# Wide tiles in the first feed-forward: two chunks of one image per operation of ScalarE, VectorE and GpSimd

## The reference, cut to what matters

```python
def _L0_conv_ref(x, gn_w, gn_b, w1, b1, w2, b2):
    # fft and inverse fft cancel; group norm with 8 groups, weight and bias
    xn = groupnorm(x, 8) * gn_w + gn_b
    h = relu(einsum('oc,bchw->bohw', w1, xn) + b1)
    return x + einsum('oc,bchw->bohw', w2, h) + b2

x = x + _L0(_gn(x))     # first feed-forward: the change is here
x = x + _L1(_gn(x))     # four sweeps: row by row, new = row + relu(conv9(prev) + b)
x = x + _L2(_gn(x))     # four sweeps
x = x + _L3(_gn(x))     # attention over channels, second feed-forward with gelu
```

## Time and profile before

| | |
|---|---|
| median of 3 runs | 2603.39 us |
| the profiled execution | 2601.79 us |
| its span, first to last instruction | 2600.0 us |
| TensorE busy | 2508.5 us (96%) |
| VectorE busy | 1809.3 us (70%) |
| ScalarE busy | 1238.0 us (48%) |
| GpSimd busy | 357.4 us (14%) |
| convolutions of the sweeps (line 883) | 2199.5 us, 40640 matmul records |
| granted TensorE clock, mean | 0.991 of full speed |

### The profile page before, as it was taken

The page is one execution under the profiler, slowest core; times in us unless marked ns, Lnnn a source line. Parts: engine busy times, 40 slices in busy tenths (PEclk is TensorE's granted clock), DMA queues, the critical chain, the costliest instruction groups (busy, mean ns, idle before and its releaser), DMA issues. The chain is left out here.

```text
span 2600.0 us, 116999 instructions
## 1 busy us (share of the span) xinstructions
PE 2508.5 (96%) x46072; PEld 2415.1 (93%) x46072; DVE 1809.3 (70%) x5768; ACT 1238.0 (48%) x2705; POOL 357.4 (14%) x551
## 2 busy tenths in 40 slices
PE   1999999999999999999999999999999999998998
PEld 1389999999999999999899999999999999997885
DVE  7866666666666666677666666666666666777986
ACT  0866663222233333377666642222333333676877
POOL 1610000000000000066100000000000000653545
PEclk9999999999999999999999999999999999998999
DMA  7810001222450000087700012223700000430006
GB/s 271 222 42 0 0 0 38 61 61 61 92 52 0 0 5 0 0 259 162 198 1 0 0 29 61 61 61 87 68 0 0 0 0 0 130 97 2 4 4 259
DMA packets 323834, 155.07 MB, mean 60 GB/s; under 512 B 155169, under 2 KB 319650, under 8 KB 319650
## 3 DMA queue, kind: packets, MB, share of 16 engines
q1 hardware_dynamic: 321600, 153.41, 23.1%
q10 hardware_dynamic: 2146, 0.53, 0.1%
HBM read 70.00 MB, written 50.33 MB: 46 GB/s over the span
## 5 line engine op out<-in xcount | busy, mean ns | idle before, releaser
L883 PE MATMUL banks<-x_row,w_taps 128*64 128x124 f32 (+2 forms) x40640 | 2199.5, 270 | 4.4 <-DVE x_row L1128 3.1
L883 PEld LDWEIGHTS banks<-x_row,w_taps 128*64 128x64 f32 x40640 | 2197.4, 135 | 6.5 <-issue 4.7
L1137 DVE SCALAR_TENSOR_TENSOR x_row<-banks,sweep_nbias,biased_row 128x128 f32<-128x128 f32 x2032 | 713.3, 351 | 713.1 <-PE banks L883 686.0
L668 ACT ACTIVATE biased_row<-state,sweep_bias 128x256 f32 (+1 forms) x762 | 512.8, 673 | 1038.3 <-DVE state L1140 605.2
L664 ACT ACTIVATE biased_row<-state,aff,gn_a 128x64 f32 (+1 forms) x1016 | 364.6, 430 | 183.4 <-DVE state L1146 179.6
L1140 DVE SCALAR_TENSOR_TENSOR state<-banks,sweep_nbias,biased_row 128x128 f32 (+1 forms) x1016 | 444.4, 437 | 0.0
L553 POOL TENSOR_TENSOR state<-state,stripe_a 128x256 f32<-128x256 f32 x96 | 66.9, 735 | 1979.6 <-DVE state L1140 1959.3
L1146 DVE SCALAR_TENSOR_TENSOR turn_ring<-banks,sweep_nbias,biased_row 128x64 f32<-128x64 f32 x1016 | 237.1, 275 | 0.0
L1146 DVE SCALAR_TENSOR_TENSOR state<-banks,sweep_nbias,biased_row 128x64 f32 (+1 forms) x1016 | 237.1, 275 | 0.0
L856 PE MATMUL banks<-res,ffn_w 64*64 64x512 f32 x512 | 112.3, 597 | 6.1 <-ACT res L603 5.2
L845 PE MATMUL banks<-state,ffn_s 64*64 64x512 f32 x512 | 107.1, 601 | 0.3 <-DVE ffn_s L1300 0.3
(11 more groups left out here) (139 smaller groups left out, 904.0 us busy)
## 6 DMA issues: line engine op xcount, KB each, us to landing
state<-turn_ring SPq DMA_DIRECT2D x512, 64.0 KB, 1.9
resid<-state SPq DMA_DIRECT2D x94, 256.0 KB, 3.6
state<-x_in SPq DMA_DIRECT2D x16, 1024.0 KB, 20.6
stripe_a<-resid SPq DMA_DIRECT2D x32, 512.0 KB, 5.4
stripe_b<-resid SPq DMA_DIRECT2D x32, 512.0 KB, 5.4
out_y<-state SPq DMA_DIRECT2D x16, 1024.0 KB, 4.0
res<-resid SPq DMA_DIRECT2D x32, 256.0 KB, 7.3
resid<-state SPq DMA_DIRECT2D x16, 512.0 KB, 6.5
```

The costliest lines, as they stand in the source:

```text
L668: nc.scalar.activation(as_cells(n, biased_row[:, k, :, :]), cells(n, slice(0, B), i, k, g), ACT.Identity, bias=sweep_bias[:, n:n + 1]).the ...
L883: last = nc.tensor.matmul(out_ps[blk, :, lo:hi], w_taps[:, n % 2, s, blk], x_row[c][src][:, :, s + lo:s + hi], start=at == 0, stop=at == T ...
L1137: nc.vector.scalar_tensor_tensor(x_row[c][par][:, :, 2:2 + HALF], ps, nb, br, ALU.max, ALU.add).then_inc(row_ready[c], 1)
```

## The change

Two chunks of one image are now one tile of 1024 columns: `wide_tile(t)` with t = 4 (pair of chunks) + image, 32 tiles (`WIDE`) in place of 64. Its first product lies in the two banks of `pair[t % 2]`, the second in those of `pair[2 + t % 2]`, its hidden part in `hid_wide[:, t % 2]`. TensorE still makes matmuls of 512 columns, eight for each wide tile, up(t) before down(t - 1); down(t) waits for the addition of tile t - 2. ScalarE, GpSimd and VectorE make one operation where they made two, except bn_stats, which stays at 512 columns, twice. The first pair of chunks gets bn_stats for all images (before, the first chunk). SyncE waits for the four images of a pair and then issues the eight stores of its two chunks. All loops of this feed-forward are written out. The second feed-forward keeps its narrow tiles; its counts are shifted.

```diff
+    WIDE = B * CHUNKS // 2
+        hid_wide = hid.rearrange("p b n -> p (b n)").rearrange("p (u n) -> p u n", u=2)
+        squares_wide = stripe_a[:].rearrange("p (u n) -> p u n", u=2)
+        def wide_tile(t):
+            return half_rows[:, t // B * 4 * CR:(t // B + 1) * 4 * CR, t % B, :]
@@ sync
-            with sp.Fori(0, CHUNKS) as j:
-                sp.wait_ge(ffn_added, j * B + B)
+            for j in range(CHUNKS):
+                if j % 2 == 0:
+                    sp.wait_ge(ffn_added, (j // 2 + 1) * B)
                 store_residual_a(j)
@@ gpsimd
+                for t in range(WIDE):
+                    pool.wait_ge(ffn_up_done, t + 1)
+                    xs, b = wide_tile(t), t % B
+                    nc.gpsimd.tensor_scalar(xs, xs, a1[:, b:b + 1], cb[:, b:b + 1], ALU.mult, ALU.add).then_inc(x_scaled_by_pool, 1)
@@ scalar
+                def relu(t):
+                    act.wait_ge(ffn_up_done, t + 1)
+                    nc.scalar.activation(hid_wide[:, t % 2, :], pair[t % 2][:], ACT.Relu, bias=ffn1_b[:, t % B:t % B + 1]).then_inc(hidden_ready, 1)
+                def square(j, b):
+                    act.wait_ge(ffn_added, j * B + b + 1)
+                    act.wait_ge(shift_ready, 1)
+                    if j > 1:
+                        act.wait_ge(ffn_squares_summed, j * 2 + (b - 5))
+                    nc.scalar.activation(squares_wide[:, b - 2, :].rearrange("p (r w) -> p r w", w=WH), wide_tile(j * B + b), ACT.Square,
+                                         bias=minus_shift[:, b:b + 1], accum_out=sums[:, 1, b, j:j + 1]).then_inc(ffn_squares_summed, 1)
+                for j in range(CHUNKS // 2):
+                    for b in range(B):
+                        relu(j * B + b)
+                        if j > 1 and b in (1, 2):
+                            square(j - 1, b + 1)
+                for b in (2, 3):
+                    square(CHUNKS // 2 - 1, b)
@@ tensor
+                def up(t):
+                    b = t % B
+                    for k in range(2):
+                        j = t // B * 2 + k
+                        for q in range(2):
+                            src, dst = slice(q * C, (q + 1) * C), half_of(q, k)
+                            last = nc.tensor.matmul(pair[t % 2][dst, k * BANK:(k + 1) * BANK], ffn1_s[src, b, src],
+                                                    half_rows[src, j * 2 * CR:(j + 1) * 2 * CR, b, :], start=True, stop=True)
+                    last.then_inc(ffn_up_done, 1)
+                def down(t):
+                    pe.wait_ge(hidden_ready, t + 1)
+                    if t >= 2:
+                        pe.wait_ge(ffn_added, t - 1)
+                    for k in range(2):
+                        for q in range(2):
+                            src, dst = half_of(q, k), slice(q * C, (q + 1) * C)
+                            last = nc.tensor.matmul(pair[2 + t % 2][dst, k * BANK:(k + 1) * BANK], ffn2_w[src, 0, src],
+                                                    hid_wide[src, t % 2, k * BANK:(k + 1) * BANK], start=True, stop=True)
+                    last.then_inc(ffn_down_done, 1)
+                up(0)
+                for t in range(1, WIDE):
+                    up(t)
+                    down(t - 1)
+                down(WIDE - 1)
@@ vector
+                def add(t):
+                    j, b = t // B, t % B
+                    dve.wait_ge(x_scaled_by_pool, t + 1)
+                    dve.wait_ge(ffn_down_done, t + 1)
+                    xs = wide_tile(t)
+                    ps = pair[2 + t % 2][:].rearrange("p (r w) -> p r w", w=WH)
+                    if j and b in SUMMED:
+                        nc.vector.scalar_tensor_tensor(xs, ps, 1.0, xs, ALU.mult, ALU.add,
+                                                       accum_out=sums[:, 0, b, j:j + 1]).then_inc(ffn_added, 1)
+                        return
+                    nc.vector.tensor_tensor(xs, ps, xs, ALU.add).then_inc(ffn_added, 1)
+                    dve.wait_ge(ffn_added, t + 1)
+                    for k in range(2):
+                        nc.vector.bn_stats(stats[:, b, 2 * j + k, :], tile_of(2 * j + k, b)).then_inc(dve_link, 1)
+                    chain[0] += 2
```

More of the change, by code:

```diff
@@ L594, in _, with ffn_wide @@
             root(3, bank[7])
[L596 to L600, removed]
+            def ffn_wide():
+                act.wait_ge(coefs_ready, 1)
+                def relu(t):
                     act.wait_ge(ffn_up_done, t + 1)
[L603 to L607, removed]
+                    nc.scalar.activation(hid_wide[:, t % 2, :], pair[t % 2][:], ACT.Relu, bias=ffn1_b[:, t % B:t % B + 1]).then_inc(hidden_ready, 1)
                 def square(j, b):
@@ L620, in chunk, with ffn, tile @@
+                for b in (2, 3):
+                    square(CHUNKS // 2 - 1, b)
+            ffn_wide()
+            def ffn():
+                act.wait_ge(coefs_ready, 5)
+                def tile(j, b):
+                    act.wait_ge(ffn_up_done, j * B + (b + WIDE + 1))
+                    nc.scalar.activation(hid[:, b, :], bank[b], ACT.Gelu, bias=ffn1_b[:, b:b + 1]).then_inc(hidden_ready, 1)
+                with act.Fori(0, CHUNKS) as j:
                     tile(j, 0)
                     tile(j, 1)
-                    if layer:
-                        scale(j)
@@ L635, in ffn @@
[L635 to L641, removed]
             def rows(n):
@@ L870, in ffn @@
                 down(CHUNKS - 1, 3)
-            ffn(0)
+            ffn_wide()
             def conv(n, c, k, hcount):
@@ L981, in _ @@
             keep_warm(WARM_BLOCK)
-            ffn(1)
+            ffn()
         @block.vector
@@ L1062, in _, with ffn @@
             nc.vector.tensor_scalar(ffn1_b[:], bank[6][:, 0:B], b1, None, ALU.add).then_inc(coefs_ready, 1)
[L1064 to L1074, removed]
+            def ffn():
+                with dve.Fori(0, CHUNKS) as j:
+                    for b in range(B):
+                        if b == 0:
+                            dve.wait_ge(x_scaled, j + 1)
+                        else:
+                            dve.wait_ge(x_scaled_by_pool, j * (B - 1) + (WIDE + b))
+                        dve.wait_ge(ffn_down_done, j * B + (WIDE + b + 1))
+                        xs = tile_of(j, b)
+                        nc.vector.tensor_tensor(xs, bank[B + b].rearrange("p (r w) -> p r w", w=WH), xs, ALU.add).then_inc(ffn_added, 1)
@@ L1077, in add @@
                         return
                     nc.vector.tensor_tensor(xs, ps, xs, ALU.add).then_inc(ffn_added, 1)
[L1079 to L1087, removed]
@@ L1094, in ffn @@
                 link(ins)
                 nc.vector.tensor_scalar(minus_shift[:, 2:4], mv[:, 2:4, 0], -1.0, None, ALU.mult).then_inc(shift_ready, 1)
-                link(nc.vector.tensor_scalar(first_tile[:], mv[:, 2:4, :].rearrange("p b s -> p s b"), 1.0 / CHUNKS, None, ALU.mult))
-                with dve.Fori(1, CHUNKS) as j:
-                    for b in range(B):
-                        add(j, b, b in SUMMED)
-                chain[0] += (CHUNKS - 1) * (B - len(SUMMED))
+                link(nc.vector.tensor_scalar(first_tile[:], mv[:, 2:4, :].rearrange("p b s -> p s b"), 2.0 / CHUNKS, None, ALU.mult))
@@ L1101, in ffn @@
+                for t in range(B, WIDE):
+                    add(t)
                 dve.wait_ge(dve_link, chain[0])
@@ L1302, in _ @@
             ins.then_inc(coefs_ready, 1)
-            ffn(1, False)
+            ffn()
 def kernel(**inputs):
```

59 lines of the change are left out of this document (25 added, 34 removed).

## The result

The changed kernel takes 2620.69 us (median of 4 runs, 2619.40 to 2621.89), the kernel before in the same series 2603.18 (4 runs): 17.5 us slower, ratio 1.0068 [1.0055, 1.008]. Forecast were 2605.1 us and no measurable change. The first feed-forward, on which the whole argument was spent, went as forecast within a microsecond. The time was lost 2400 us later, in the second feed-forward.

A forecast was written before the change was run, and what follows sets the result against it. TensorE's sweeps fill nearly all the time, and the first feed-forward's stores release the first sweep. Release -0.9 and cold clock +2.6 sum to +1.7 us, giving 2605.1 us; own range 2602 to 2608, 8 in 10 for 2600.5 to 2609.5.

The forecast's parts named there:

- The step that failed: Second feed-forward: no longer writing out its first chunk was priced at nothing, hidden under its matmuls.
- the three rivals: Alternatives: stores already at their limit (chance 0.2), wide tiles save nothing (0.08), stores not the limit (0.1).
- The arithmetic of the first feed-forward: First feed-forward: rounds of 7.5 us against 8.78, last addition at 125.9 against 134.1, gaining nearly 8 us.
- 0.2 us late at the round: First feed-forward, change of round: product reaches its addition 0.2 us late because two PSUM pairs replace four banks.
- tail +0.4: End of the first feed-forward: 0.4 us longer, as ScalarE's last wide square ends after the aggregation.
- The stores: First feed-forward's writes to resid: they hide the arithmetic gain and release the first sweep at 140.1 against 140.98.
- The rate of 250 GB/s: First feed-forward stores in 1 KB pieces: assumed speed, so 16.78 MB take 67.1 us.
- the term -0.9: Start of the first sweep: stores release it at 140.1 instead of 140.98, 0.9 us sooner.
- The lower bound of 236 GB/s: First feed-forward stores: slowest rate assumed, from the steady state, giving release at 144.1.
- rival 1: First feed-forward stores already at their limit, 236 to 240 GB/s: +4.5 to +6.4 us, about 2609; chance 0.2.
- rival 3: First feed-forward stores are not the limit, arithmetic sets the end: about 2600.4 us; chance 0.1.
- The clock: Start of the first sweep: TensorE, idle some 7 us, resumes at half clock, costing 2.6 us (bounds 0 and 3.7).

The follow-up runs named there:

- e2_loop: Kernel before, narrow tiles kept, with only ScalarE's loop of the second feed-forward started at chunk 0; 2616.49 us, ratio 1.0052.
- e1_peel: Changed kernel with the first chunk of the second feed-forward written out again ahead of ScalarE's loop; 2605.65 us, ratio 1.0012.
- e10_primer: Changed kernel, loop still from 0, with a tiny Gelu into a scratch column ahead of ScalarE's second feed-forward loop; 2605.03 us, ratio 1.0011.
- e8_unroll: Kernel before with the first feed-forward's loops of ScalarE, VectorE and SyncE written out, tiles narrow, stores as before; 2599.19 us, ratio 0.9984.
- e6_rows: e1_peel with each first feed-forward chunk stored as one 1 MB transfer in 8 KB pieces, rows exchanged by later loads; 2596.11 us, ratio 0.9975.
- e3_warm: e1_peel with 26 unread TensorE products filling the first sweep's wait for the stores; 2603.35 us, ratio 1.0003.

## Why the prediction was wrong

**The step that failed** is the sentence that "ffn() of the last block changes only in that its first chunk is no longer written out, which I price at nothing, under its matmuls". It was worth +14 us: 13.9 alone in e2_loop, and without it the changed kernel takes 2605.65 (e1_peel) or 2605.03 (e10_primer), where the forecast was 2605.1. The matmuls could not hide it. ScalarE had 0.30 us of idle time a chunk there, and the load takes 1.28. The profile of before had the instruction in one row, a load x1 at the line of the Gelus; the question that was not asked is where the one load stood. It stood at the first Gelu of the chunk that was written out ahead of the loop. None of the three rivals had anything to do with it, nor did the range hold it.

**The arithmetic of the first feed-forward** was right within half a microsecond: first store 71.4 (71.43), 2.48 and 1.14 us an addition (2.47, 1.13), 0.2 us late at the round (0.22), round 7.5 (7.49), last addition 125.9 (125.44), tail +0.4 (0.43). x_row is scaled by 132.15 (forecast 132.3). In part this is luck. The slopes of ScalarE and VectorE were both taken between two unlike instructions: VectorE's came out (1.14 for 1.13 us), ScalarE's did not (1.00 for 1.11). And the first addition came at 62.84, not 62.5. Both errors were hidden or made up for later. The durations outside the loop had been taken for the right reason, as e8_unroll shows.

**The stores** set the release, as forecast, and swallow the whole gain. The rate of 250 GB/s was right, 253 behind the hole of 80 to 82 us; it was the hole that the forecast lacked. It let the bytes flow from 72.7 without a break, though by its own numbers the second pair was ready more than 9 us after the first (71.2, then 73.4 and a round of 7.5) and a pair written in 8.4. The hole is some 0.7 of the 0.9 us between 140.1 and 141.0; the term -0.9 was 0.0. The lower bound of 236 GB/s, on which rival 1 rests, was not a limit of the DMA engines but the pace of VectorE (e8_unroll above). The 341 and 425 GB/s that rival 3 sets against it are, in the Trainium skill (DMA: Bandwidth & Descriptors, "Measured"), of loads from HBM into SBUF and say nothing of stores; the stores here reach 406 GB/s in e6_rows. Of rival 3, e6_rows also shows the price that the prediction could not: with stores that are not the limit the step comes 8.2 us sooner.

**The clock** cost 2.74 us in the trace and 2.3 in the runs of e3_warm (forecast 2.6). The Trainium skill (TensorE: Matmul & The Clock Gate, "HAM oscillation") has half of the throttled time as the penalty: from the first step at 142.55 to the end of the cold stretch at 148.5 this is 3.0, near the 2.74 of the trace, if the part of the 9.75 us that passes in the wait is left out. Release and clock together are +2.7 in the trace, and the runs of e1_peel show +3.0, against a forecast of +1.7.

**Open, and what one trace can carry:** executions of the same code differ by as much as some of these terms. e2_loop is the kernel before until its second feed-forward, and e10_primer has the changed kernel's first feed-forward. The third step of e2_loop, and the release in e10_primer:

```profile
145.88 0.35 DVE L1137 SCALAR_TENSOR_TENSOR x_row<-banks,sweep_nbias,biased_row 128x128 f32<-128x128 f32 x1 [0.88 <-PE banks L883]
```

```profile
143.46 2.76 ACT L675 ACTIVATE biased_row<-state,aff,gn_a 128x64 f32<-128x64 f32 x8 [10.73 <-DMA resid<-state]
```

The former is 1.6 us later than in the kernel before (144.29), with the clock at 1.2 GHz until about 145 us and not 141.25; the latter is 2.5 us later than in the changed kernel (141.00; e1_peel has 141.47). So a difference of one or two us between two traces is not yet a cause, and the terms of the release and the clock are known only to about that; the costs of the edits above rest on the medians. The same holds for a further 2 us that the after profile loses between 1814 and 2365, with a granted clock of 0.96 from 1806 to 1849 where before has 1.00: e1_peel has the 0.96 too, e10_primer the 1.00. What decides it in an execution is not known.

## What to carry to other kernels

Before a loop is made to start at its first pass, look for what the pass written out had set up. Here the table load was executed once where it stood ahead of the loop, and 16 times where it stood within it. An operation of a few elements that uses the same table, placed ahead of the loop in idle time, keeps it out. And where a transfer sets the end of a stage, price the faster arithmetic together with the shape of the transfer, and with the moment at which the first one can start: the wide tiles and the other stores each came to nothing alone and to 6.7 us together, while the loops written out, which leave the first store nearly where it was, gained 3.7 us on the old stores.

## What the hardware showed

- A table load takes 1283 ns in all of the 16 passes, also in the 15 that follow a Gelu, whose table is then in place.
- Stores in pieces of 1 KB: 248 GB/s at a share of 0.91. In pieces of 8 KB, with one transfer where there were four: 269 GB/s at 0.65, with gaps between chunks, and 406 GB/s at 0.98 while the queue is full. The number of transfers changed with the piece; which of them it is was not separated.
- With the loops of ScalarE, VectorE and SyncE written out, VectorE's bn_stats follows its addition by 0.73 us and not 0.84, and a chunk of four tiles is 0.28 us shorter.
- Operations of 1024 columns over two banks: ScalarE 1.11 us, GpSimd 1.20, VectorE 1.22. ScalarE's was forecast at 1.00, by a slope between two instructions of which only one reads a bias; one slope has to come from one form.
